# A down-projection by Strassen's seven products, with its weights streamed through a ring of four

## The reference, cut to what matters

```python
mod = swish(c) @ w_mod + b_mod                      # six rows of 576 for each of the two batches
xn  = ln(x) * (1 + sc_msa) + sh_msa
q, k, v = heads(xn @ w_qkv + b_qkv)                 # 16 heads of 36
o   = softmax(ln(q) @ ln(k).T / 6) @ v
x   = x + g_msa * (o @ w_proj + b_proj)
xn2 = ln(x) * (1 + sc_mlp) + sh_mlp
h   = gelu(xn2 @ w1 + b1)                           # [2, 2048, 2304]
x   = x + g_mlp * (h @ w2 + b2)                     # w2 is [2304, 576]
```

## Time and profile before

| | us |
|---|---|
| median of 3 runs (lowest, highest) | 2652.15 (2650.34, 2652.68) |
| the profiled execution's own time | 2651.53 |
| span of its records | 2649.7 |
| granted clock of TensorE, mean over the span | 0.999 |
| TensorE busy with matmuls | 2611.8 (99% of the span) |
| VectorE, ScalarE, GpSimd busy | 1647.1, 1467.4, 469.4 |
| bytes moved by DMA | 179.10 MB, 68 GB/s on average |

### The profile page before, as it was taken

One profiled execution on the slowest core, in us unless ns is written; L12 is line 12 of the kernel. 1 busy time (PEld: TensorE's weight loads), 2 busy tenths in 40 slices (PEclk: granted clock), 3 DMA queues, 4 the chain that ended last, 5 costly groups with the idle time before them and its releaser, 6 DMA issues.

```text
span 2649.7 us, 42010 instructions
## 1 busy us (share of the span) xinstructions
PE 2611.8 (99%) x15820; PEld 1318.7 (50%) x15820; DVE 1647.1 (62%) x2677; ACT 1467.4 (55%) x2174; POOL 469.4 (18%) x339
## 2 busy tenths in 40 slices
PE   6999999999999999999999999999999999999999
PEld 3444444444444444444444334375757575666657
DVE  7788887788888788888888512344343535353421
ACT  4787787777777788788788786412121211111110
POOL 2532332222222222222222100110101010010100
PEclk9999999999999999999999999999999999999999
DMA  7513311133332123333333322402020211202000
GB/s 234 95 36 79 79 36 35 46 74 72 69 73 50 46 70 81 73 78 81 78 79 84 99 77 91 157 15 96 18 79 26 70 60 37 72 24 84 13 19 19
DMA packets 257862, 179.10 MB, mean 68 GB/s; under 512 B 172745, under 2 KB 211087, under 8 KB 256953
## 3 DMA queue, kind: packets, MB, share of 16 engines
q1 hardware_dynamic: 257370, 176.37, 25.0%
q10 hardware_dynamic: 288, 0.04, 0.0%
HBM read 96.49 MB, written 41.06 MB: 52 GB/s over the span
## 4 chain that ended last, share of the span: by engine, by line
PE 94%; DMA 1%; DVE 1%; SPq 1%; ACT 1%; issue 1%; POOL 0%; DVEq 0%; ACTq 0%
PE at_ps L1864 19%; PE at_ps L1200 18%; PE at_ps L1183 17%; PE at_ps L1890 14%; PE at_ps L1237 11%; PE at_ps L1211 8%; PE at_ps L1220 4%; PE at_ps L1883 1%; PE at_ps L1826 1%; PE at_ps L1843 1%; DMA ml_held<-head_rden 1%; PE at_ps L1261 1%; PE at_ps L1918 0%; DMA st_wm_first<-in_L_cond_b_mod 0%; SPq L486 0%
## 5 line engine op out<-in xcount | busy, mean ns | idle before, releaser
L755 ACT ACTIVATE at_p<-at_ps 128x1024 f32<-128x1024 f32 x1024 | 1040.0, 1029 | 330.9 <-PE at_ps L1183 326.3
L1200 PE MATMUL at_ps<-at_p,at_v 128*37 128x512 f32 x2304 | 590.3, 592 | 0.0
L935 DVE TENSOR_TENSOR at_rest_of_p<-at_p,at_pr 128x1024 bf16<-128x1024 f32 x448 | 553.0, 1234 | 15.4
L623 POOL TENSOR_TENSOR at_tssq<-at_tssq,power 128x8 f32<-128x8 f32 x112 | 276.7, 2470 | 880.6 <-DVE at_tssq L899 879.9
L1864 PE MATMUL at_ps<-ml_w2s,ml_hid 128*128 128x288 f16 x3348 | 414.9, 286 | 0.0
L1890 PE MATMUL at_ps<-ml_xhi,ml_w 128*128 128x512 f16 x1296 | 382.0, 379 | 0.0
L1864 PEld LDWEIGHTS at_ps<-ml_w2s,ml_hid 128*128 128x128 f16 x3348 | 327.5, 98 | 82.0
L1211 PE MATMUL at_ps<-at_pr,at_vr 128*101 128x512 f32 x896 | 365.1, 489 | 1.3 <-DVE at_pr L927 1.2
L927 DVE CAST at_pr<-at_p 128x1024 fp32r<-128x1024 f32 x448 | 314.6, 702 | 81.0 <-ACT at_p L755 78.9
L1183 PE MATMUL at_ps<-at_qk_even 109*64 109x512 f16 (+1 forms) x1536 | 308.7, 382 | 3.8 <-ACT at_p L755 2.6
L1183 PE MATMUL at_ps<-at_qk_odd 109*64 109x512 f16 (+1 forms) x1658 | 308.6, 381 | 0.3 <-ACT at_p L755 0.3
(11 more groups left out here) (189 smaller groups left out, 2365.3 us busy)
## 6 DMA issues: line engine op xcount, KB each, us to landing
head_sums<-at_oT SPq DMA_DIRECT2D x256, 72.0 KB
ml_held<-head_sums SPq DMA_DIRECT2D x64, 256.0 KB
at_xy<-in_L_cond_w SPq DMA_DIRECT2D x34, 288.0 KB
w_halves<-at_wq SPq DMA_DIRECT2D x68, 144.0 KB
at_xy<-in_x SPq DMA_DIRECT2D x32, 288.0 KB, 2.8
ml_x<-in_x SPq DMA_DIRECT2D x8, 1152.0 KB, 5.4
out<-ml_x SPq DMA_DIRECT2D x7, 1152.0 KB, 4.5
ml_held<-head_rden SPq DMA_DIRECT2D x24, 216.0 KB
```

Source lines behind the costliest of these rows:

```text
L623: pool.tensor_tensor(tssq[:, 1, :], tssq[:, 1, :], keep.power[:, 0:QK], ALU.pow).then_inc(t_rstd, 1)
L755: act.activation(p[:, s % NP, :], ps[:, 2 * (s % 2):2 * (s % 2) + 2, :].rearrange("p a n -> p (a n)"), ACT.Exp).then_inc(exp_done, 1)
L935: nc.vector.tensor_tensor(rest_of_p[:, n % NL, :], p[:, s % NP, :], pr[:, n % NZ, :].bitcast(F32), ALU.subtract).then_inc(low_p_ready, 1)
L1200: last = nc.tensor.matmul(acc[a * HP:a * HP + RW, bank_of(U)], v32[:, (G % 2) * NT + 2 * s + a, h, :], p[:, s % NP, a * CH:(a + 1) * CH], ...
```

## The change: what it does

The down-projection of a chunk is the product of a matrix A (512 tokens x 2304 features) and B (2304 x 576). Both are cut into 2 x 2 blocks, tokens in two halves of 256, features in two halves of 1152 (so features f and f+9 make a pair), columns in two halves of 288. Strassen's scheme makes the four blocks of the result from seven products of sums of blocks in place of eight products of blocks. Each product is 9 pairs x 2 token tiles x 3 half-products = 54 matmuls of 288 columns.

- The seven left operands: of each pair's gelu (1024 values a partition, four quarters of 256 tokens) five sums or differences are made in f32 on VectorE (`mix`, one buffer of 5 x 256), two quarters are used as they are. ScalarE makes the high parts, in one instruction of 512 elements for the two quarters and one of 1280 for the five sums; VectorE makes the low parts, with the same two sizes.
- The seven right operands are made once, from w2 in f32, in the last group of attention (`vector_blocks`, `sync_blocks`), and stored in DRAM with w2's halves. So w2 drops out of the slices: 26 in place of 44.
- SBUF does not hold w1 and seven blocks of w2 at once. Both go through a ring of four slots (10 KB a partition each): 5 blocks of w1 and 7 of w2 for every chunk, each one DMA, its slot taken when the block four before it is used up.
- The products are folded into the result by ScalarE copies (`take`) and VectorE sums (`fold`), then gated and added to x (`finish`). The result of a chunk is finished in quarters.
- The preparation of the next chunk's attention output is tied to pairs in place of tiles: add and multiply after pairs 0, 2, 4, 5, 7, the low part after pairs 1, 3, 5, 6, 8. `high_o` now follows the high parts of the same pair as the multiply.
- The turns of the next chunk's rows come after the third, fourth and fifth product.

```diff
-    MULTIPLY_AT, HIGH_AT, LOW_AT = ({f + at: k for k, f in enumerate((1, 4, 8, 11, 14))} for at in (0, 1, 2))
-    LATE = 4
-    WITH_DOWN = ((0, 1), (2, 3), (4,), ())
+    ADD_AT, LOW_AT = ({j: k for k, j in enumerate(at)} for at in ((0, 2, 4, 5, 7), (1, 3, 5, 6, 8)))
+    TURN_WITH = {2: (0, 1), 3: (2, 3), 4: (4,)}
...
+    def load_block(self, sp, J, b):
+        n = J * BLOCKS + b
+        slot = n % RING
+        if b >= RING:
+            self.block_used(sp, J, b - RING)
+        elif J:
+            self.block_used(sp, J - 1, b + BLOCKS - RING)
...
+        sp.dma_start(self.ring[:, slot, 0:width], src).then_inc(self.ring_loaded[slot], 16)
...
     def scalar(self, act):
         def gelu(J, f):
-            m = J * FT + f
+            m, n = J * FT + f, J * PAIRS + f // 2
             act.wait_ge(self.up_ready, m + 1)
-            act.wait_ge(self.hlo_ready, m + 1)
-            act.activation(self.g32[:, f % 2, :], self.up_bank(f), ACT.Gelu_apprx_tanh, bias=self.b1col[:, f:f + 1],
+            if n >= 2 and f % 2 == 0:
+                act.wait_ge(self.hlo_ready, 2 * n - 2)
+            act.activation(self.g32[:, n % 2, (f % 2) * CH:(f % 2 + 1) * CH], self.up_bank(f), ACT.Gelu_apprx_tanh, bias=self.b1col[:, f:f + 1],
                            scale=1.0 / WS).then_inc(self.gelu_done, 1)
+        def high(J, j):
+            n = J * PAIRS + j
+            act.wait_ge(self.gelu_done, 2 * n + 2 + 2)
+            act.copy(self.hid[:, 5:7, j, 0, :], self.quarters(n)[:, 0:4:3, :]).then_inc(self.hhi_ready, 1)
+            act.wait_ge(self.mixed, 3 * n + 3)
+            act.copy(self.hid[:, 0:5, j, 0, :], self.mix[:, :, :]).then_inc(self.hhi_ready, 1)
...
-            for f in range(FT):
-                gelu(J, f)
-                if more and f in self.HIGH_AT:
-                    self.high_o(act, J + 1, self.HIGH_AT[f])
+            for j in range(PAIRS):
+                gelu(J, 2 * j)
+                gelu(J, 2 * j + 1)
+                high(J, j)
+                if more and j in self.ADD_AT:
+                    self.high_o(act, J + 1, self.ADD_AT[j])
+            take(J, 0, self.part[:, 1, :].rearrange("p (i n) -> p i n", i=2), TPC * (J + 2) if more else TPC * (J + 1), 4 * J)
+            take(J, 1, self.corner[:, :, :], 0, 4 * J)
...
+        def hidden(J, j):
+            n = J * PAIRS + j
+            q, mix, hid = self.quarters(n), self.mix, self.hid
+            dve.wait_ge(self.gelu_done, 2 * n + 2 + 2)
+            if n:
+                dve.wait_ge(self.hlo_ready, 2 * n)
+            nc.vector.tensor_tensor(mix[:, 0:2, :], q[:, 0:2, :], bcast(q[:, 3, :], 1, 2), ALU.add).then_inc(self.mixed, 1)
+            nc.vector.tensor_tensor(mix[:, 2:4, :], q[:, 1:3, :], q[:, 0:4:3, :], ALU.subtract).then_inc(self.mixed, 1)
+            nc.vector.tensor_tensor(mix[:, 4, :], q[:, 0, :], q[:, 2, :], ALU.add).then_inc(self.mixed, 1)
+            dve.wait_ge(self.hhi_ready, 2 * n + 1)
+            nc.vector.tensor_tensor(hid[:, 5:7, j, 1, :], q[:, 0:4:3, :], hid[:, 5:7, j, 0, :], ALU.subtract).then_inc(self.hlo_ready, 1)
+            dve.wait_ge(self.hhi_ready, 2 * n + 2)
+            nc.vector.tensor_tensor(hid[:, 0:5, j, 1, :], mix[:, :, :], hid[:, 0:5, j, 0, :], ALU.subtract).then_inc(self.hlo_ready, 1)
...
+            def finish(of, n, a, h):
+                cols = slice(h * HALF, (h + 1) * HALF)
+                rows = self.x1[:, (J % 2) * TPC + 2 * a:(J % 2) * TPC + 2 * a + 2, cols]
+                dve.wait_ge(self.down_step, step + n - 1)
+                fold(of, of, bcast(self.gates[:, J // NCH, 1, cols], 1, 2), ALU.mult)
+                dve.wait_ge(self.down_step, step + n)
+                nc.vector.tensor_tensor(rows, rows, of, ALU.add).then_inc(self.out_ready, 1)
...
+            fold(v, v, M(6), ALU.add)
+            finish(v, 12, 0, 0)
...
+            for j in range(PAIRS):
+                hidden(J, j)
+                if J == 0 and j == PAIRS // 2:
                     self.invert_den(dve, 1)
-                if more and f in self.MULTIPLY_AT:
-                    self.add_o(dve, J + 1, self.MULTIPLY_AT[f])
-                    self.multiply_o(dve, J + 1, self.MULTIPLY_AT[f])
-                if more and f in self.LOW_AT:
-                    self.low_o(dve, J + 1, self.LOW_AT[f])
+                if more and j in self.ADD_AT:
+                    self.add_o(dve, J + 1, self.ADD_AT[j])
+                    self.multiply_o(dve, J + 1, self.ADD_AT[j])
+                if more and j in self.LOW_AT:
+                    self.low_o(dve, J + 1, self.LOW_AT[j])
...
         def project(J, r0):
             pe.wait_ge(self.olo_ready, KC * (J + 1))
+            if J > 1:
+                pe.wait_ge(self.down_step, 12 * (J - 1))
...
+        def down(J, turn):
+            for idx in range(7):
+                w = self.block(pe, J, W1_BLOCKS + idx).rearrange("p (j h n) -> p j h n", j=PAIRS, h=2)
+                if idx == 0:
+                    pe.wait_ge(self.gelu_done, FT * (J + 1) + 2)
+                if idx in (1, 2) and turn:
+                    pe.wait_ge(self.pair_taken, TPC * (J + 2) - 2 + idx)
+                if idx == 1 and not turn:
+                    pe.wait_ge(self.down_step, 12 * J)
+                if idx in (3, 4):
+                    pe.wait_ge(self.m_copied, 3 * J + idx - 2)
+                if idx >= 4:
+                    pe.wait_ge(self.down_step, 12 * J + (1, 3, 7)[idx - 4])
+                for j in range(PAIRS):
+                    if idx == 0:
+                        pe.wait_ge(self.hlo_ready, 2 * (J * PAIRS + j + 1))
+                    h = self.hid[:, A_OF[idx], j, :, :]
+                    for i in range(2):
+                        t = slice(i * P, (i + 1) * P)
+                        for n, (a, b) in enumerate(((0, 0), (0, 1), (1, 0))):
+                            last = nc.tensor.matmul(self.m_banks(idx)[:, i, :], h[:, a, t], w[:, j, b, :],
+                                                    start=(j == 0 and n == 0), stop=(j == PAIRS - 1 and n == 2))
+                last.then_inc(self.m_done, 1)
+                if turn and idx in self.TURN_WITH:
+                    self.turn_y(pe, J + 1, self.TURN_WITH[idx])
```

More of the change, by code:

```diff
@@ L531, in store_slice @@
             def store_slice(i):
-                src, half, r0, cols = slices[i]
-                n = src.shape[0]
-                for h, part in enumerate((word_hi, word_lo)):
-                    sp.dma_start(half[h, r0:r0 + n, cols].rearrange("p (a n) -> p a n", a=2), part[0:n]).then_inc(w_stored, 16)
+                src, _, places = slices[i]
+                for to, part in zip(places, word_of(i)[1:]):
+                    sp.dma_start(to, part[0:src.shape[0]]).then_inc(w_stored, 16)
             def unit(G, u):
@@ new lines, in block_used, with block, sync_blocks @@
+    def block_used(self, sp, J, b):
+        if b < W1_BLOCKS:
+            sp.wait_ge(self.up_ready, J * FT + min(4 * b + 4, FT))
+        else:
+            sp.wait_ge(self.m_done, J * 7 + b - W1_BLOCKS + 1)
+    def block(self, pe, J, b):
+        n = J * BLOCKS + b
+        pe.wait_ge(self.ring_loaded[n % RING], 16 * (n // RING + 1))
+        return self.ring[:, n % RING, :]
+    def sync_blocks(self, sp, u):
+        if 1 <= u <= PAIRS:
+            sp.wait_ge(self.w2_step, 4 * u)
+            for half, part in enumerate((self.w2_hi, self.w2_lo)):
+                sp.dma_start(self.halves.w2[:, :, u - 1, half, :].rearrange("m p n -> p m n"), part[:, :, :]).then_inc(self.w2_stored, 16)
+        if u < PAIRS:
+            if u == 0:
+                sp.wait_ge(self.ends.low_p_used, self.ends.all_splits)
+            if u >= 2:
+                sp.wait_ge(self.w2_step, 4 * u - 4)
+            for k in range(2):
+                f = u + k * PAIRS
+                sp.dma_start(self.w2_in[:, u % 2, 2 * k:2 * k + 2, :].rearrange("p a n -> p (a n)"), self.w2[f * P:(f + 1) * P, :]).then_inc(self.w2_in_loaded, 16)
@@ L1577, in sync @@
         sp.wait_ge(self.ends.pv_done, self.UNITS_DONE * STEPS + 1)
+        sp.wait_ge(self.w2_stored, 32 * PAIRS)
         self.load_den(sp, 1)
-        self.load_w2(sp)
-        for J in range(self.CHUNKS - 1):
-            self.load_x(sp, J + 1)
-            self.load_sums(sp, J + 1, (2, 3, 4))
+        for J in range(self.CHUNKS):
+            more = J + 1 < self.CHUNKS
+            if J:
+                store(J - 1)
+            if more:
+                self.load_x(sp, J + 1)
+                self.load_sums(sp, J + 1, (2,))
+            self.load_block(sp, J, 4)
+            if more:
+                self.load_sums(sp, J + 1, (3,))
+            self.load_block(sp, J, 5)
+            if more:
+                self.load_sums(sp, J + 1, (4,))
             if J == 0:
@@ L1654, in gelu, with take @@
                            scale=1.0 / WS).then_inc(self.gelu_done, 1)
-        act.wait_ge(self.b1_loaded, 16)
+        def high(J, j):
[4 more added lines that the diff above has]
```

(31 more changed lines are left out.)

248 lines of the change are left out of this document (156 added, 92 removed).

## The result

| | before | after |
|---|---|---|
| median, us (lowest, highest) | 2651.24 (2650.17, 2652.68) | 2764.8 (2763.05, 2766.13) |
| span of the profiled execution | 2649.7 | 2764.1 |
| mean granted clock of TensorE | 0.999 | 0.971 |
| start of up, chunk 0 | 1680.4 | 1743.0 |
| up to up, chunks 1 to 6, mean | 122.35 | 129.85 |

The kernel is slower: 1.0428 times the time before, 95% interval 1.0409 to 1.0446. Forecast were 2703 us in 2670 to 2735, so the direction was right and the size was not: +112.7 us on the 2652.15 from which the forecast started, against its +50.8.

A forecast was written before the change was run, and what follows sets the result against it. TensorE, busy 2611.8 of 2649.7 us, was taken as the bound. -52.9 +71.4 +12.4 +0.7 +1.7 +17.5 = +50.8 us on 2652.15 gave 2703 us, range 2670 to 2735.

The forecast's parts named there:

- the first of the edits costed at nothing: Last attention group: making w2's seven operands fits VectorE's spare time, and SyncE's stores have a unit's slack; 0 us.
- The matmuls left out, -52.9: Down on TensorE: 54 fewer matmuls a chunk at 0.1225 us, 6.62 us a chunk, 52.9 over 8.
- The stall ahead of project, 11.9 us a chunk: TensorE waits after up for the last attention low part, queued behind pair 8; +71.4 us over chunks 1 to 6.
- Chunk 0, +12.4: Project in chunk 0 starts at up+68.9 in place of up+56.55, including the inversion of the denominators; +12.4 us.
- Chunk 7, +0.7 and +1.7: Last chunk: first product waits for the gelu of f = 17, +0.7; longer final VectorE instructions and store, +1.7 us.
- The clock, 2.5 us a stall: TensorE's clock drops after each of seven stalls before project; 2.5 us each, +17.5 us, bounds 0 and 3.3 each.
- The ring, 0: Block loads of w1 and w2 through four slots arrive in time; taken 0, other end +96 us at twice the duration.
- A: Rival: ScalarE and VectorE keep up with TensorE in the chunk, stall only 5.8 us; 2642 us, chance 0.06.
- B: Rival: stalls before project as worked out, but TensorE's clock held at 2.4 GHz; 2685 us, chance 0.22.
- C: Rival: the DMA queue gives ring blocks late, up to +96; 2740 to 2800 us, chance 0.07.
- D: Rival: half the stall before project, 7 to 8 us; 2672 us, or 2655 with clock held, chance 0.1.
- The range: Whole kernel: 2670 to 2735 us, from B and part of D to handshakes 0.3 us longer at 17 steps a chunk.

The follow-up runs named there:

- the loop opened: Changed kernel with w2's quarters loaded one unit earlier and VectorE's w2 work behind add and multiply in the last attention group: 2718.2 us (1.0256).
- the kernel with six edits: Kernel with all four edits, plus ring block 5 loaded behind piece 4's sums and the five sums' high and low parts in two pieces: 2614.36 us (0.9859).
- all four edits: Changed kernel: w2 quarters earlier, VectorE's w2 work behind multiply, `high_o` behind next pair's gelus, attention pieces after pairs 0, 2, 3, 5, 6: 2638.23 us (0.9957).
- the two edits of the second stage: Changed kernel with `high_o` behind the next pair's gelus and attention's add and multiply after pairs 0, 2, 3, 5, 6: 2686.47 us (1.0136).

## Why the prediction was wrong, step by step

- **The step that failed** is the first of the edits costed at nothing: "The seven operands of w2: VectorE is busy for 27.2 of 180 us in the last group of attention; about 6 us in each of 9 units of 10 us leaves room. SyncE waits there for VectorE before its next stores; these have a unit's slack." The last group got 62.6 us longer. The room is there, as VectorE's 73.5 of 243 us show. The slack isn't: store, load, sums, high, low and store again are one loop over SyncE, a DMA queue and VectorE, 16.4 us long in the turn shown against a unit of 10.3, and it stands in VectorE's program ahead of a multiply for which ScalarE waits ahead of its exponentials. I argued from a busy sum a few paragraphs below the one that refuses such an argument for the chunk ("Throughput would do ... The order of the programs does not do"). The prediction's own question, what is queued behind the waiting instruction, was not put to this wait. The runs return 46.0 us with the loop opened. The ring's first four blocks, another term put at nothing, give 5.6 more when they are issued behind w2's stores; for 11 us the runs show ScalarE's waits and not what makes the stores late. With the last group at 62.6 in place of 0 the sum would have been 113.4, on a measured 114.4.
- **The matmuls left out, -52.9: right.** 3024 matmuls of down; the kernel with six edits shows 6.62 us a chunk as such.
- **The stall ahead of project, 11.9 us a chunk: right.** A row of the waits of the second stage, and three of its groups by form, two of which the trace of before had not:

```profile
PE at_ps L2036 <- DVE ml_olo L1815: 80.5, 7, 11.5
```

```profile
L1925 DVE TENSOR_TENSOR ml_hid<-ml_mix,ml_hid 128x1280 f16<-128x1280 f32 x72 | 107.4, 1492 | 52.1 <-ACT ml_hid L1774 52.1
L1774 ACT CAST ml_hid<-ml_mix 128x1280 f16<-128x1280 f32 x72 | 90.6, 1258 | 94.1 <-DVE ml_mix L1921 94.1
...
L1737 ACT CAST ml_ohi<-ml_held 128x512 f16<-128x512 f32 x35 | 21.6, 618 | 103.1 <-DVE ml_held L1810 103.1
```

  11.5 a chunk for 11.9; 1258 and 1492 ns for 1.26 and 1.48 us from slopes; 103.1/35 = 2.95 before `high_o` for 2.9. The timeline of chunk 2, whose up starts at 2009.23:

```profile
2016.49 0.69 DVE L1919 TENSOR_TENSOR ml_mix<-ml_g 128x512 f32<-128x512 f32 x1 [4.89 <-ACT ml_g L1766]
...
2022.30 0.62 ACT L1737 CAST ml_ohi<-ml_held 128x512 f16<-128x512 f32 x1 [2.89 <-DVE ml_held L1810]
...
2024.12 0.69 DVE L1919 TENSOR_TENSOR ml_mix<-ml_g 128x512 f32<-128x512 f32 x1 [1.85 <-ACT ml_g L1766]
```

  The first pair's sums start at up+7.26 (forecast 7.3), the second's 7.63 later (7.63). Project starts at 2074.58, up+65.35 (65.4).
- **Chunk 0, +12.4: 2.1 short.** The first sums wait for a store of attention's last output, which lands at 1753.5 (VectorE is idle for 21.1 us before them), and start at up+10.8 in place of 8.7; project starts at up+70.96 in place of 68.9.
- **Chunk 7, +0.7 and +1.7: 0.5 short**, -3.7 for -4.2.
- **The clock, 2.5 us a stall: right.** Windows of the kernel after, at the start of project in chunk 2:

```profile
2074.00:2076.00 2.00, 1.42 (x7) 0.89 (x7) 0.52 (x1) 0.00 (x0) 0.00 (x0) 0.50 0.00 0
2080.00:2082.00 2.00, 2.00 (x18) 1.60 (x17) 1.49 (x2) 0.00 (x0) 0.00 (x0) 1.00 0.00 0
```

  After 11.5 us without work the granted clock is 0.50, the lower level of 1.2 GHz, and back at 1.00 from 2080. Project takes 16.08, in chunk 0 16.69 and in the last 15.89 us for 13.73 without a stall (the chain of the kernel with six edits): 2.2 to 3.0 lost, 16.7 in all for 17.5. The stalls of 5.85 us in the kernel with `high_o` behind the gelus drop it to 0.50 as well, and project takes 15.23 to 16.80 there, though these stalls are all of one length. With all four edits the waits are 1.6 to 3.9 us. Behind the four up to 2.24 the clock stays at 1.00 and project takes 13.91; behind 2.71, 2.76 and 3.92 it falls, and project takes 15.4 to 15.6:

```profile
1991.50:1993.50 2.00, 2.00 (x17) 1.60 (x18) 2.00 (x4) 0.53 (x1) 0.00 (x0) 1.00 1.03 435
2110.00:2112.00 2.00, 1.93 (x9) 1.22 (x10) 2.00 (x5) 0.42 (x1) 0.00 (x0) 0.50 0.98 415
```

  What the clock costs there is part of the 118.5 us of its chunks. The length of the wait alone does not decide it: with the two edits of the second stage alone the clock falls behind waits of 2.01 and 2.21 us and stays behind 1.95. In the kernel after, it falls at each of the seven stalls. This is what the Trainium skill says (TensorE: Matmul & The Clock Gate, "HAM oscillation — how this bites in real kernels"): a recurring wait makes every stretch behind it start slow, not the first alone. The trace of the kernel after agrees, seven times out of seven; with all four edits it is three of seven. In the last group the clock's mean is 0.88, and the forecast had no term for that: TensorE's work takes 13.0 us longer there, which are part of the 62.6.
- **The ring, 0: right for the chunks of the change as it is**, and wrong for a better order of it and for its first four blocks, as above. Rivals A, B, C and D did not happen; none of them was about the last group. The range was built from the second stage's unknowns alone.

## What to carry to other kernels

Work put into the "spare time" of an engine that runs in order costs by its waits, not by its busy time: add up the loop that feeds it (issue, landing, work, store, issue again), compare it with the period it has to fit, and follow what stands behind the waiting instruction, engine by engine. A step costed at nothing deserves the same working as the one that looks expensive. Where two engines hand an operand to and fro and set the pace, two smaller instructions can be faster than one large (124.7 us a chunk for 129.85 here), and a wait that feeds another engine's next tile belongs behind that tile's work.

## What the runs showed of the hardware that I had not expected

The two loads of b1, 1152 single elements each, hold SyncE for 9.75 us at their issue, where two loads of 288 KB take 3.53 (the timeline at 1547.46) and two of 128 single elements 1.16. Of the 9.75 the first load has 0.99 and the second 8.71. The kernel before loads the same column with one DMA of 2304 elements, issued in 0.43 us, and there the issue behind it takes 5.42. So the length of an issue is not set by its own elements alone; whether the number of elements or the full queue holds SyncE is not told apart here.

```profile
1518.35 9.75 SPq L1654 DMA_DIRECT2D ml_b1col<-in_L_cond_b  x2
```

The same place in the kernel before:

```profile
1518.23 0.43 SPq L1562 DMA_DIRECT2D ml_b1col<-in_L_cond_b  x1
1524.57 5.42 SPq L518 DMA_DIRECT2D head_sums<-at_oT  x1
```

A ring block of 1296 KB lands 6.2 us after its issue (the median of 56 in the kernel after). A store of 504 KB takes 14.95 us behind four blocks of 1152 KB, and 4.5 where these come later: a small DMA behind large ones is late by theirs, though the mean over the span is 105 GB/s.
